# Right-hand matrix loaded before Wv, its casts on GpSimd, its scales spread by two fp32 matmuls, and the FFN of two chunks ahead of V

## The chip, the cores and the metric

The kernel runs on all 8 cores of one Trainium2 chip, each with its own 4096 tokens; the cores don't exchange data. The metric is the device time of the slowest core in microseconds. A profile beside it shows one execution on each core; the numbers below are of its slowest core, 6, where nothing else is said.

## The reference

For x of 16 sequences x 2048 tokens x 1024 features:

```python
xn = _layernorm(x, axis=-1)                       # no gain, no bias
s = _L0_attn_ref(xn, Wq, Wk, Wv, Wo)              # 16 heads of 64, causal window of 128 keys
lhs_scale = absmax(xn, each row) / 127;  rhs_scale = absmax(rhs, each column) / 127
q_lhs = round(xn / lhs_scale);  q_rhs = round(rhs / rhs_scale)     # int8
g = _silu((q_lhs @ q_rhs) * lhs_scale * rhs_scale)
x = x + s * g
```

(The lines on the scales are shortened from the reference's helpers.)

## The kernel before, in words

A core treats its 4096 rows as 32 chunks c of 128 rows (two sequences of 16 chunks). Names of PE groups, with chunk or pair s = c // 2 and half h or quarter g:

- TX: eight 128x128 transposes of the normalized chunk `xnr` into `xnt` (chunks 0 to 5; later chunks are transposed by DMA). TL: the same for the quantized chunk `qlr` into `qlt` (chunks 0 to 3). TR: the same for one 128-row strip of the quantized right-hand matrix into `qrhs` (8 strips).
- Q, K: four quarters for a pair of chunks, 16 matmuls of 256 columns each. V, F, O: two halves for a chunk, 8 matmuls of 512 columns each; F is the product with `qrhs` (the FFN), O the output projection.
- S, A: scores, and probabilities times V, of a chunk in four slots b. Before S of a slot comes the exponential of the slot before (one score buffer `psc`); before A comes the mask on VectorE.

`pe_order` writes PE's order out by hand: a start-up part, then for each chunk four slots, with the groups of `slot_gaps(c)` between the slots. The other engines' programs are written out beside it in the same order of events; each engine runs strictly in order, with semaphores between them. From chunk 2 on, every chunk repeats one pattern.

Around the change. The host passes the right-hand matrix transposed (`rhst`), so a strip i of 128 output columns has its scale in one row each: `rabs(i)` is an absolute maximum over a 128x1024 strip (VectorE), `rscale(i)` four small operations for two strips, `rq(i)` the scaling and rounding on ScalarE, in place, `rcast(i)` the cast to bf16 on VectorE, then TR(i) and its two evacuations. Strips are staged in tiles that the steady loop uses later (`xr`, `gg`, `zz`, `tt`), and cast into `aot`/`ao`. The scales come out one per partition, but `zev` (evacuation of F, `zz<-pj,sm,rsb`) needs them along the free axis in all partitions: `load_rs` writes them to DRAM (`rs_scratch`) and reads them back broadcast into `rsb`. Weights are loaded and cast by DMAs that GpSimd issues (`load_w`: 8 of 256 KB landed, 512 KB read); x and the strips by DMAs of SP's queue. `rstd(c)` is six small GpSimd operations, on which `xn(c)` (normalization, VectorE) waits. `cen(c)`, `amax(c)`, `qp(c)`, `ql(c)` quantize a chunk on ScalarE and VectorE in turn.

Of the kernel before, what the change touches and what calls it, by code (L numbers as in the profile page):

```python
# [890 lines left out]
```

How the kernel before makes its waits and increments, by code:

```python
        def op(fn, sem=None, tag=None, n=1):  # L165
            if tok[0].emit:
                i = fn()
                if sem is not None:
                    i.then_inc(S[sem], n)
            if sem is not None:
                tok[0].add(sem, n, tag)
# [1 line left out]
        def need(eng, sem, tag):  # L173
            if tok[0].emit:
                eng.wait_ge(S[sem], tok[0].named[(sem, tag)])
# [1 line left out]
        def landed(eng, sem, nth):  # L177
            if tok[0].emit:
                eng.wait_ge(S[sem], 16 * (nth + 1))
# [1 line left out]
        def own(eng, sem):  # L181
            if tok[0].emit:
                eng.wait_ge(S[sem], tok[0].count[sem])
```

## Time and profile before

| | |
|---|---|
| time, median of 3 runs | 723.78 us (722.06 to 723.83) |
| time of the profiled execution | 726.37 us |
| its span, slowest core | 724.8 us (cores 721.8 to 724.8) |
| PE busy | 662.3 us, 91% of the span |
| VectorE, ScalarE, GpSimd busy | 470.6, 349.0, 167.5 us |

The time covers a little more than the span of the slowest core. PE's busy share is an average: a stretch of the start and the steady part have to be read apart. The page's slices show the granted TensorE clock in tenths of full speed: 9s nearly everywhere, lower digits only in the first 130 us.

### The profile page before, as it was taken

What the parts mean: (1) busy time and instruction counts of PE and PEld (TensorE: products, weight loads), DVE (VectorE), ACT (ScalarE), POOL (GpSimd) and SP (SyncE); (2) the same over time, 40 slices, a digit from 0 to 9 for tenths busy, and PEclk for the clock granted to TensorE, in tenths of its full rate; (3) what the DMA queues carried; (4) which work ended last, traced back from release to release, by engine and by line L of the source; (5) the groups of instructions that cost most, each with busy time, mean ns of one, the idle gap of its engine ahead of it and who ended that gap; (6) DMA issues with size and microseconds to landing.
All of it is one profiled execution on the core that took longest, in us unless ns stands there. A gap on an engine that the chain in (4) does not pass through costs nothing.

```text
span 724.8 us, 16874 instructions; the slowest of 8 cores (721.8 to 724.8 us)
## 1 busy us (share of the span) xinstructions
PE 662.3 (91%) x5655; PEld 414.1 (57%) x5720; DVE 470.6 (65%) x955; ACT 349.0 (48%) x479; POOL 167.5 (23%) x291
## 2 busy tenths in 40 slices
PE   2879662999999999999999999999999999999985
PEld 2665331666665656666666556566666665656642
DVE  4644651777777667766767766677666677664485
ACT  2634631544455555555445545455554455554442
POOL 7312000132221221222222212112222221220122
PEclk9989976899999999999999999999999999999999
DMA  9999703385454455755544644666465445542343
GB/s 189 183 190 242 133 1 72 74 168 128 109 87 116 113 130 132 132 118 131 129 105 79 117 128 117 131 132 132 117 132 124 99 92 114 121 96 74 74 93 141
DMA packets 111043, 86.92 MB, mean 120 GB/s; under 512 B 93168, under 2 KB 93296, under 8 KB 110960
## 3 DMA queue, kind: packets, MB, share of 16 engines
q1 hardware_dynamic: 106064, 77.35, 47.6%
q0 software_dynamic: 4608, 8.39, 7.7%
q8 instruction: 48, 0.79, 0.5%
q14 instruction: 35, 0.29, 0.2%
q10 hardware_dynamic: 288, 0.10, 0.1%
HBM read 55.15 MB, written 16.78 MB: 99 GB/s over the span
## 4 chain that ended last, share of the span: by engine, by line
PE 81%; DMA 6%; DVE 5%; issue 4%; POOL 2%; ACT 1%; DVEq 0%; POOLq 0%; SPq 0%; ACTq 0%
PE pj L661 42%; PE pj L652 28%; PE psc L743 5%; PE pav L767 4%; DMA xs<-x 2%; DMA rsb<-rs_scratch 2%; PE pav L769 2%; DMA rs_scratch<-sm 2%; DVE ee L353 1%; DVE sm L288 1%; DVE sm L403 1%; POOL wk L811 1%; POOL sm L791 0%; DVE xnr L318 0%; DVE ao L366 0%
## 5 line engine op out<-in xcount | busy, mean ns | idle before, releaser
L559 ACT ACTIVATE ee<-psc 128x1024 bf16<-128x1024 f32 (+1 forms) x128 | 128.3, 1003 | 163.8 <-PE psc L743 153.1
L806 POOL TENSOR_TENSOR xr<-tt,xr 128x512 f32<-128x512 f32 x63 | 80.4, 1278 | 369.4 <-DVE tt L391 338.7
L652 PE MATMUL pj<-xnt,wk 128*128 128x256 bf16 x1024 | 119.6, 277 | 5.0 <-ACT kt L542 4.5
L652 PE MATMUL pj<-xnt,wq 128*128 128x256 bf16 x1024 | 119.8, 276 | 2.2 <-ACT qt L542 1.1
L661 PE MATMUL pj<-qrhs,qlt 128*128 128x512 bf16 x482 | 117.5, 387 | 2.9 <-DVE qrhs L308 1.2
L661 PE MATMUL pj<-wv,xnt 128*128 128x512 bf16 x482 | 115.5, 383 | 1.9 <-issue 0.2
L661 PE MATMUL pj<-wo,aot 128*128 128x512 bf16 x507 | 115.8, 379 | 1.5 <-ACT aot L310 1.2
L353 DVE TENSOR_TENSOR ee<-ee,mask_s 128x1024 bf16<-128x1024 bf16 (+1 forms) x128 | 102.9, 804 | 15.4 <-ACT ee L559 5.9
L652 PEld LDWEIGHTS pj<-xnt,wk 128*128 128x128 bf16 x1024 | 99.6, 99 | 17.7 <-issue 5.4
L652 PEld LDWEIGHTS pj<-xnt,wq 128*128 128x128 bf16 x1024 | 99.4, 99 | 15.1 <-issue 2.9
L661 PEld LDWEIGHTS pj<-wo,aot 128*128 128x128 bf16 x512 | 49.6, 98 | 59.8 <-issue 1.5
L661 PEld LDWEIGHTS pj<-qrhs,qlt 128*128 128x128 bf16 x512 | 48.5, 99 | 55.2 <-issue 4.6
L391 DVE TENSOR_TENSOR tt<-pj,gg 128x512 f32<-128x512 f32 x64 | 44.0, 690 | 53.9 <-PE pj L661 52.7
L525 ACT ACTIVATE xs<-xs,sm 128x1024 f32<-128x1024 f32 x32 | 36.7, 1148 | 83.7 <-DVE xnr L318 83.7
L661 PEld LDWEIGHTS pj<-wv,xnt 128*128 128x128 bf16 x512 | 48.2, 98 | 48.4 <-issue 1.7
L377 DVE SCALAR_TENSOR_TENSOR zz<-pj,sm,rsb 128x512 f32<-128x512 f32 x64 | 47.8, 747 | 30.4 <-DMA rsb<-rs_scratch 20.9
L366 DVE TENSOR_TENSOR ao<-pav,sm 128x256 bf16<-128x256 f32 x128 | 54.4, 425 | 17.9 <-DVE sm L364 5.9
L767 PE MATMUL pav<-vv,ee 128*128 128x65 bf16 x480 | 47.1, 197 | 18.9 <-DVE ee L353 18.3
L323 DVE TENSOR_REDUCE sm<-xs 128x1 f32<-128x1024 f32 x32 | 38.9, 1217 | 35.0 <-ACT xs L525 35.0
L743 PEld LDWEIGHTS psc<-qt,kt 64*128 64x128 bf16 x992 | 28.4, 95 | 51.3 <-issue 51.0
L743 PE MATMUL psc<-qt,kt 64*128 64x128 bf16 x992 | 50.6, 221 | 4.1 <-ACT ee L559 4.1
L767 PEld LDWEIGHTS pav<-vv,ee 128*128 128x128 bf16 x480 | 32.6, 98 | 32.0 <-issue 20.4
(76 smaller groups left out, 616.0 us busy)
## 6 DMA issues: line engine op xcount, KB each, us to landing
xs<-x SPq DMA_DIRECT2D x32, 512.0 KB, 5.6
xr<-x SPq DMA_DIRECT2D x32, 512.0 KB, 6.4
y<-xr SPq DMA_DIRECT2D x31, 512.0 KB, 7.3
wq<-wqt POOLq DMA_DIRECT2D x8, 256.0 KB, 15.5
wk<-wkt POOLq DMA_DIRECT2D x8, 256.0 KB, 19.4
wv<-wvt POOLq DMA_DIRECT2D x8, 256.0 KB, 22.5
xr<-rhst SPq DMA_DIRECT2D x4, 512.0 KB, 7.2
wo<-wot POOLq DMA_DIRECT2D x8, 256.0 KB, 9.7
```

Of the source, the lines that this page charges most:

```text
L323: op(lambda: v.reduce_max(col(c, AMAX), xs[c % XS][:], AX.X, apply_absolute_value=True), "v")
L353: op(lambda: v.tensor_tensor(a, a, m, ALU.mult), "v", ("mask", c, b))
L366: op(lambda: v.tensor_tensor(view(ao[c % 2], b * 256, (64, 4), (1, 64)), view(p, 0, (66, 4), (1, 64)), bass.AP(sm, C_RS + 4 * (b % 2), [[1 ...
L377: op(lambda: v.scalar_tensor_tensor(zz[h], banks[bank["F", c, h]], col(c, LSH), rsb[:, h * 512:(h + 1) * 512], ALU.mult, ALU.mult), "v", ( ...
L391: op(lambda: v.tensor_tensor(tt[h], banks[bank["O", c, h]], gg[c % 2][:, h * 512:(h + 1) * 512], ALU.mult), "v", ("ev", "O", c, h))
L525: op(lambda: a.activation(xs[c % XS][:], xs[c % XS][:], AF.Identity, scale=-1.0, bias=col(c, MEAN)), "a", ("cen", c))
L559: op(lambda: a.activation(o, i, AF.Exp, scale=0.125), "a", ("exp", c, b))
L652: yield [(lambda kc=kc, m=m: t.matmul(p[:, m * 256:(m + 1) * 256], w[:, kc * 1024 + (2 * j + m) * 128:kc * 1024 + (2 * j + m + 1) * 128], ...
L661: yield [lambda kc=kc: t.matmul(p[:], src[:, off + kc * step:off + kc * step + 128], w[:, kc * 1024 + j * 512:kc * 1024 + (j + 1) * 512], ...
L743: todo.append(lambda m=m, kk=kk, ko=ko, rows=rows, q0=q0: t.matmul(psc[:, q0:q0 + 128], kk[rows, m * 256 + ko:m * 256 + ko + 128], qt[s % ...
L767: todo.append(lambda out=out, e0=e0, vp=vp: t.matmul(out, e[:, e0:e0 + 128], vp, start=True, stop=False))
L806: op(lambda: p.tensor_tensor(r, tt[h], r, ALU.add), "p", ("add", c, h))
```

## The change

The work is the same but for the way the scales are spread. What moves:

- SP's queue loads only x of chunks 0 to 3 first, then, once the sixth piece of Wk has landed, the eight strips, then x of chunks 4 to 6.
- GpSimd issues four pieces of Wq before the first `rstd`s and the rest in between; it casts the strips (`rcast`), and issues Wv in two fours between the casts, and Wo after the casts and `rstd(5)`.
- The scales: `rdiag` writes the identity matrix times the scales (diagonal blocks) into `rsb`, a matmul with a matrix of ones sums over the partitions (RS, one for each half), and ScalarE copies the sum over `rsb`.
- PE's order: TR 0 to 3, RS, half 0 of F for chunks 0 and 1, then TR 4 to 7, RS, half 1, all ahead of V. The slots of chunks 0 and 1 hold V of chunks 4 and 5 alone.
- Chunks 4 and 5 are centred and quantized later.

```diff
@@ slot_gaps
-    if c == 0:
-        return [[g] + halves("TR", i) for i, g in enumerate(halves("V", 4, 5))]
-    if c == 1:
-        return [halves("TR", 4, 5), halves("TR", 6, 7) + halves("F", 0)[:1], halves("F", 0, 1)[1:3], f[1:]]
+    if c < 2:
+        v = halves("V", c + 4)
+        return [v[:1], [], v[1:], []]
@@ pe_order
-    out += one(ks("Q", 1)) + one(halves("TL", 0))
-    out += [("G", ks("K", 0), range(8))]
-    out += one(ks("K", 1)) + one(halves("TL", 1, 2))
-    out += [("G", halves("V", 0, 1), range(8))] + one(halves("TX", 4) + halves("V", 2))
-    out += one(halves("TX", 5) + halves("TL", 3) + halves("V", 3))
+    out += one(ks("Q", 1)) + one(halves("TL", 0, 1))
+    out += [("G", ks("K", 0), range(8))] + one(halves("TL", 2))
+    out += one(ks("K", 1)) + one(halves("TL", 3))
+    for h in range(2):
+        out += one(halves("TR", *range(4 * h, 4 * h + 4)) + [("RS", 0, h), ("F", 0, h), ("F", 1, h)])
+    out += [("G", halves("V", 0, 1), range(8))]
+    out += one(halves("TX", 4) + halves("V", 2) + halves("TX", 5) + halves("V", 3))
@@ staging
-        stage = [xr[0], xr[1], xr[2], gg[0], gg[1], zb, tb]
-        rst_bf = [aot[0], aot[1], ao[1]]
+        stage = [gg[0], gg[1], zb, tb, xr[0], xr[1], xr[2], tb]
+        rst_bf = [aot[0], aot[1], ao[0], ao[1]]
@@ emit_sync
-            for c in range(6):
+            for c in range(4):
                 load_x(sync, c)
-            landed(sync, "wv4", 0)
+            landed(sync, "wk5", 0)
             for i in range(8):
                 load_rh(sync, i)
-            t_ql(sync, 4)
-            t_ql(sync, 5)
-            load_x(sync, 6)
-            load_rs(sync)
+            for c in range(4, 7):
+                load_x(sync, c)
@@ VectorE: rcast goes, rdiag is new
+        def rdiag(v, h):
+            need(v, "v", ("rsc", 4 * h + 2))
...
+            op(lambda: v.tensor_tensor(view(rsb, h * 512, (128, 4), (1, 128)), view(ident, 0, (0, 4), (1, 128)),
+                                       bass.AP(sm, C_RST + 4 * h, [[192, 128], [1, 4], [0, 128]]), ALU.mult),
+               "v", ("rdiag", h))
@@ ScalarE
+            elif k == "RS":
+                need(a, "t", g)
+                op(lambda: a.copy(rsb[:, h * 512:(h + 1) * 512], banks[bank[g]]), "a", ("ev",) + g)
@@ PE
+            if k == "RS":
+                yield [lambda: t.matmul(p, ones[:], rsb[:, j * 512:(j + 1) * 512], start=True, stop=True)]
@@ GpSimd
+        def rcast(p, i):
+            need(p, "a", ("rq", i))
+            if i >= 4:
+                need(p, "t", ("TR", i - 4, 1))
+            op(lambda: p.tensor_scalar(rst_bf[i % 4][:], stage[i][:], -MAGIC, 1.0, ALU.add, ALU.mult),
+               "p", ("rcast", i))
```

Three places of the engines' orders. GpSimd, first of the kernel before, from the `rstd` of chunk 3 over Wv to the first operation of chunk 4:

```order
L789 TENSOR_SCALAR sm<-sm 128x1
L791 TENSOR_TENSOR sm<-sm 128x1
L793 TENSOR_TENSOR sm<-sm 128x1
L795 TENSOR_TENSOR sm<-sm 128x1
L797 TENSOR_SCALAR sm<-sm 128x1
L799 TENSOR_TENSOR sm<-sm 128x1
L811 DMA wv<-wvt 128x1024 x8
L789 TENSOR_SCALAR sm<-sm 128x1
```

and of the changed kernel, after the `rstd` of chunk 3 (L839 is `rcast`, L816 the first operation of `rstd(4)`):

```order
L845 DMA wk<-wkt 128x1024 x5
L839 TENSOR_SCALAR aot<-gg 128x1024 x2
L845 DMA wv<-wvt 128x1024 x4
L839 TENSOR_SCALAR ao<-zz 128x1024
L839 TENSOR_SCALAR ao<-tt 128x1024
L845 DMA wv<-wvt 128x1024 x4
L839 TENSOR_SCALAR aot<-xr 128x1024 x2
L839 TENSOR_SCALAR ao<-xr 128x1024
L839 TENSOR_SCALAR ao<-tt 128x1024
L816 TENSOR_SCALAR sm<-sm 128x1
```

Wv now stands behind casts, which wait for ScalarE; before, nothing but `rstd(3)` stood ahead of it.

PE of the kernel before, from K to the first TR (transposes have `ident_s`; L743 is S, L769 A):

```order
L652 MATMUL pj<-xnt,wk 128x256 x128
L646 MATMUL psc<-ident_s,qlr 128x128 x8
L646 MATMUL pav<-ident_s,qlr 128x128 x8
L661 MATMUL pj<-wv,xnt 128x512 x32
L646 MATMUL psc<-ident_s,xnr 128x128 x8
L661 MATMUL pj<-wv,xnt 128x512 x16
L646 MATMUL pav<-ident_s,xnr 128x128 x8
L646 MATMUL psc<-ident_s,qlr 128x128 x8
L661 MATMUL pj<-wv,xnt 128x512 x16
L743 MATMUL psc<-qt,kt 128x128 x4
L661 MATMUL pj<-wv,xnt 128x512 x8
L646 MATMUL pj<-ident_s,aot 128x128 x8
```

and of the changed kernel, from TR(3) to V of chunks 0 and 1 (L666 is RS, `pj<-qrhs,qlt` F):

```order
L671 MATMUL psc<-ident_s,ao 128x128 x8
L666 MATMUL pav<-rsb,ones_s 128x512
L686 MATMUL pj<-qrhs,qlt 128x512 x16
L671 MATMUL pav<-ident_s,aot 128x128 x4
L671 MATMUL psc<-ident_s,aot 128x128 x8
L671 MATMUL pav<-ident_s,aot 128x128 x4
L671 MATMUL pav<-ident_s,ao 128x128 x4
L671 MATMUL psc<-ident_s,ao 128x128 x8
L671 MATMUL pav<-ident_s,ao 128x128 x4
L666 MATMUL pav<-rsb,ones_s 128x512
L686 MATMUL pj<-qrhs,qlt 128x512 x16
L686 MATMUL pj<-wv,xnt 128x512 x32
```

TR, RS and four halves of F now lie between K and V; before, they lay between the slots of chunks 0 and 1.

SP's queue of the kernel before, from its start to the first load of the residual x:

```order
L202 DMA xs<-x 128x1024 x6
L246 DMA xr<-rhst 128x1024 x3
L246 DMA gg<-rhst 128x1024 x2
L246 DMA zz<-rhst 128x1024
L246 DMA tt<-rhst 128x1024
L246 DMA xr<-rhst 128x1024
L223 DMA_TRANSPOSE qlt<-qlr 128x8x128 x2
L202 DMA xs<-x 128x1024
L250 DMA rs_scratch<-sm 128x8x1
L253 DMA rsb<-rs_scratch 128x1024
L229 DMA_TRANSPOSE aot<-ao 128x8x128
L209 DMA xr<-x 128x1024
```

and of the changed kernel:

```order
L203 DMA xs<-x 128x1024 x4
L247 DMA gg<-rhst 128x1024 x2
L247 DMA zz<-rhst 128x1024
L247 DMA tt<-rhst 128x1024
L247 DMA xr<-rhst 128x1024 x3
L247 DMA tt<-rhst 128x1024
L203 DMA xs<-x 128x1024 x3
L224 DMA_TRANSPOSE qlt<-qlr 128x8x128
L230 DMA_TRANSPOSE aot<-ao 128x8x128
L210 DMA xr<-x 128x1024
```

The two transfers by way of `rs_scratch` are gone, and two loads of x have moved behind the strips.

## Rows read from the trace of the kernel before

**Rows 1.** Stretches of the span: length, busy time (instructions) by engine, granted clock, DMA share, GB/s.

```profile
36.00:50.00 14.00, 9.49 (x76) 7.85 (x77) 8.50 (x19) 6.04 (x9) 3.48 (x12) 0.88 1.06 177
50.00:58.00 8.00, 8.00 (x64) 6.56 (x63) 0.02 (x1) 2.63 (x5) 0.00 (x0) 0.78 1.04 264
58.00:75.00 17.00, 16.60 (x104) 8.39 (x104) 10.08 (x18) 8.57 (x15) 4.34 (x8) 1.00 1.05 216
112.00:126.00 14.00, 0.00 (x0) 0.00 (x0) 1.82 (x5) 1.08 (x2) 0.00 (x0) 0.61 0.48 94
200.00:690.00 490.00, 487.44 (x4213) 303.86 (x4262) 333.74 (x668) 248.09 (x340) 110.97 (x180) 1.00 0.53 113
```

**Rows 2.** The chain that ended last: start us, us, what.

```profile
94.53 14.62 DMA rs_scratch<-sm
109.22 14.69 DMA rsb<-rs_scratch
```

**Rows 3.** Timeline of PE: start us, us, line, operation [idle before <- releaser].

```profile
27.92 7.15 PE L652 MATMUL pj<-xnt,wq 128*128 128x256 bf16 x64 [1.14 <-ACT qt L542]
47.65 10.00 PE L652 MATMUL pj<-xnt,wk 128*128 128x256 bf16 x64 [4.51 <-ACT kt L542]
58.79 6.85 PE L661 MATMUL pj<-wv,xnt 128*128 128x512 bf16 x31 [0.25 <-issue]
...
74.08 0.29 PE L743 MATMUL psc<-qt,kt 64*128 64x128 bf16 x4
...
103.79 3.19 PE L661 MATMUL pj<-qrhs,qlt 128*128 128x512 bf16 x7 [1.23 <-DVE qrhs L308]
...
107.89 3.74 PE L661 MATMUL pj<-qrhs,qlt 128*128 128x512 bf16 x16
...
126.30 0.22 PE L767 MATMUL pav<-vv,ee 128*128 128x65 bf16 x1 [14.35 <-DVE ee L353]
...
130.24 0.61 PE L743 MATMUL psc<-qt,kt 64*128 64x128 bf16 x8
```

**Rows 4.** Timeline of ScalarE.

```profile
45.30 1.15 ACT L525 ACTIVATE xs<-xs,sm 128x1024 f32<-128x1024 f32 x1 [1.62 <-DVE xnr L318]
...
71.35 2.21 ACT L536 ACTIVATE xr<-xr,sm 128x1024 f32<-128x1024 f32 x2
...
131.00 1.02 ACT L559 ACTIVATE ee<-psc 128x1024 bf16<-128x1024 f32 x1 [2.31 <-PE psc L743]
```

**Rows 5.** Timeline of VectorE.

```profile
41.30 0.81 DVE L318 TENSOR_SCALAR xnr<-xs,sm 128x1024 bf16<-128x1024 f32 x1
...
83.08 1.21 DVE L403 TENSOR_REDUCE sm<-zz 128x1 f32<-128x1024 f32 x1
84.40 0.17 DVE L409 TENSOR_SCALAR sm<-sm 128x2 f32<-128x2 f32 x1
...
85.01 0.17 DVE L414 TENSOR_SCALAR sm<-sm 128x2 f32<-128x2 f32 x1
...
90.48 0.68 DVE L420 TENSOR_SCALAR aot<-gg 128x1024 bf16<-128x1024 f32 x1
...
124.08 0.75 DVE L377 SCALAR_TENSOR_TENSOR zz<-pj,sm,rsb 128x512 f32<-128x512 f32 x1 [20.91 <-DMA rsb<-rs_scratch]
```

**Rows 6.** Timeline of GpSimd.

```profile
21.91 0.19 POOL L789 TENSOR_SCALAR sm<-sm 128x1 f32<-128x1 f32 x1 [2.66 <-DVE sm L290]
...
41.49 0.67 POOL L789 TENSOR_SCALAR sm<-sm 128x1 f32<-128x1 f32 x1 [1.09 <-DVE sm L290]
...
62.63 4.34 POOL L811 DMA_DIRECT2D wo<-wot  x8 [18.42 <-DMA gg<-rhst]
...
142.76 1.27 POOL L806 TENSOR_TENSOR xr<-tt,xr 128x512 f32<-128x512 f32 x1 [5.74 <-DVE sm L364]
```

**Rows 7.** Wk's loads: issue (first and last start), then time from issue to landing.

```profile
L811 POOL DMA_DIRECT2D wk<-wkt x8: 535/571/797, 12.1 to 16.0; - x8
...
DMA to landing us min/median/max: 14.3/19.4/25.9
```

**Rows 8.** Wv's loads, the same.

```profile
L811 POOL DMA_DIRECT2D wv<-wvt x8: 547/562/874, 24.4 to 28.5; - x8
...
DMA to landing us min/median/max: 18.8/22.5/25.8
```

More of the change, by code:

```diff
@@ L207, in load_xr @@
             elif c < 3:
-                need(sync, "v", ("rcast", 7))
+                need(sync, "p", ("rcast", 7))
             op(lambda: sync.dma_start(xr[c % XR][:], x_h[c * 128:(c + 1) * 128, :]), f"lr{c % XR}", c, 16)
@@ L372, in zev @@
             if c == 0:
-                landed(v, "rsr", 0)
-                need(v, "v", ("rcast", 7))
+                emptied(v, ("RS", 0, h))
+                need(v, "p", ("rcast", 3))
             else:
@@ L388, in t1 @@
             need(v, "v", ("g", c, h))
-            if c:
-                need(v, "p", ("add", c - 1, h))
+            need(v, "p", ("add", c - 1, h) if c else ("rcast", 7))
             op(lambda: v.tensor_tensor(tt[h], banks[bank["O", c, h]], gg[c % 2][:, h * 512:(h + 1) * 512],
@@ L451, in emit_vector @@
             ql(v, 0)
+            amax(v, 1)
+            ql(v, 1)
             amax(v, 2)
[L453 to L454 removed]
             evac_v(v, ("TL", 0, 0))
             ql(v, 2)
[L457 to L462 removed]
+            amax(v, 3)
             evac_v(v, ("TL", 1, 0))
+            ql(v, 3)
             evac_v(v, ("TL", 2, 0))
[L465 to L466 removed]
             rabs(v, 0)
[L468 removed]
             rabs(v, 1)
             rscale(v, 0)
[L471 to L481 removed]
+            evac_v(v, ("TL", 3, 0))
+            rabs(v, 2)
+            rabs(v, 3)
+            rscale(v, 2)
+            rdiag(v, 0)
+            evac_v(v, ("TR", 0, 0))
+            evac_v(v, ("TR", 1, 0))
+            rabs(v, 4)
+            evac_v(v, ("TR", 2, 0))
+            rabs(v, 5)
+            rscale(v, 4)
+            evac_v(v, ("TR", 3, 0))
+            rabs(v, 6)
+            zev(v, 0, 0)
+            rabs(v, 7)
+            rscale(v, 6)
+            rdiag(v, 1)
+            gate(v, 0, 0)
+            zev(v, 1, 0)
+            evac_v(v, ("TR", 4, 0))
+            evac_v(v, ("TR", 5, 0))
+            gate(v, 1, 0)
+            evac_v(v, ("TR", 6, 0))
+            evac_v(v, ("TR", 7, 0))
+            bn(v, 4)
+            zev(v, 0, 1)
+            xn(v, 4)
+            gate(v, 0, 1)
+            zev(v, 1, 1)
+            bn(v, 5)
+            xn(v, 5)
+            gate(v, 1, 1)
+            evac_v(v, ("TX", 4, 0))
+            evac_v(v, ("TX", 5, 0))
+            extra = {(0, 1): [(amax, 4)], (0, 3): [(ql, 4)], (1, 1): [(amax, 5)], (1, 3): [(ql, 5)]}
             held, gates = None, []
@@ L507, in emit_vector @@
                         ql(v, c + 4)
[L508 to L509 removed]
+                    todo = [g for g in gap if evacuator(g) == "v"]
+                    if b == 3 and todo:
                         held = todo.pop()
@@ L676, in pe_ready @@
             if k == "TR" and j == 0:
-                need(t, "v", ("rcast", i))
+                need(t, "p", ("rcast", i))
+            if k == "RS":
+                need(t, "v", ("rdiag", j))
             if k == "TA":
@@ L814, in emit_gpsimd @@
         def emit_gpsimd(p):
-            for w in range(3):
-                load_w(p, w)
-                rstd(p, 2 * w)
-                rstd(p, 2 * w + 1)
-            landed(p, "rh4", 0)
-            load_w(p, 3)
+            load_w(p, 0, range(4))
+            rstd(p, 0)
+            rstd(p, 1)
+            load_w(p, 0, range(4, 8))
+            load_w(p, 1, range(3))
+            rstd(p, 2)
+            rstd(p, 3)
+            load_w(p, 1, range(3, 8))
+            rcast(p, 0)
+            rcast(p, 1)
+            load_w(p, 2, range(4))
+            rcast(p, 2)
+            rcast(p, 3)
+            load_w(p, 2, range(4, 8))
+            for i in range(4, 8):
+                rcast(p, i)
+            rstd(p, 4)
+            rstd(p, 5)
+            load_w(p, 3, range(8))
             held = None
```

122 lines of the change are left out of this document (50 added, 72 removed).

## The prediction

> **What bounds the kernel now.** I read the stretches of the span first. From 200 to 690 us PE is busy for 487.44 of 490 us at full clock [rows 1]: the steady part is PE's, the change doesn't touch it, and what can be won lies before chunk 2. PE's timeline puts the first scores of chunk 2 at 130.24 us [rows 3]; what follows (724.8 - 130.2 = 594.6 us) I leave as it is. The question is when chunk 2 can start in the changed kernel.
>
> The chain of waits shows what holds it in the kernel before: the write of the scales to DRAM takes 14.62 us and the broadcast read back 14.69 us, one after the other from 94.53 to 123.9 us [rows 2]. The first `zev` waits 20.91 us for it [rows 5], and PE, which finds its work in the meantime until 112 us, stands still for 14.35 us [rows 3]; the stretch from 112 to 126 has no PE work at all [rows 1]. A smaller stall lies earlier: PE waits 4.51 us before K of pair 1 [rows 3], because ScalarE's `cen(4)` and `cen(5)` stand ahead of the evacuations of K and wait for late chunks of x (the last ran from 45.30 [rows 4]); after it K ran 10.00 us where the same 64 matmuls of Q took 7.15 [rows 3], with the clock at 0.78 in that stretch [rows 1]. The transfers are the other limit of the start: their share is about 1.0 through 75 us [rows 1]. Wk's last piece was issued at 16.0 and landed up to 25.9 us later, at 41.9 [rows 7]; Wv's last at 28.5 + 25.8 = 54.3 [rows 8]. Eight pieces in 12.4 us is 1.55 us for 512 KB read; I use 1.6.
>
> **The change, step by step.** I follow the longest chain from K to chunk 2, in the times of core 6.
>
> *K.* Loads of x for chunks 4 and 5 no longer share the engines with Wk: two units of 1.6 us less, of which the first strips (issued at the sixth piece) take about one back. Wk's last piece then lands at 40, K of pair 0 ends at 41 (it ended at 47.65 - 4.51 = 43.1), pair 1 starts after one evacuation, at 41.7, since `cen(4)` and `cen(5)` are behind; at Q's 7.15 us it ends at 48.9, where before it ended at 57.65. The strips 0 and 1 land by about 41, and `rabs` (1.21 us each) and `rscale` (84.40 to 85.2, 0.8 us) [rows 5] are done before 45. Beside PE, they cost nothing.
>
> *First four casts.* ScalarE's `rq(0)` stands behind the last evacuation of K, so it starts at 49.5 and takes 2.21 / 2 = 1.1 us [rows 4]; the casts start at 50.7. No row shows a GpSimd operation of 1024 columns. From below: not under the 0.68 us that VectorE needs for the same cast [rows 5], and `rq` feeds one only each 1.1 us. The nearest row is GpSimd's add of 512 columns, 1.27 us, with two inputs read [rows 6]; its 128x1 operation takes 0.19. By elements read, 1024 of one input cost the same 1.27; by elements written, 0.19 + 2 x 1.08 = 2.35, rounded up to the double of the row, 2.5. I take 1.3 us: casts 0 and 1 end at 53.3. Issuing eight pieces of weights takes 4.34 us [rows 6], so four of Wv take 2.2 and hold the casts until 55.7; casts 2 and 3 end at 58.3 (their `rq`s, after `rabs` and `rscale` behind the evacuation of TL(3), end by 55). TR(3) is done at 58.9.
>
> *RS and F, half 0.* An fp32 matmul is in no row. At least it costs the 512-column bf16 one at full clock (3.74 / 16 = 0.23 us), at most I allow four passes at half clock, 4 x 3.19 / 7 = 1.8 us [rows 3]. I take the long end, 1.7, since PE has been nearly idle since 49 us. TR(3)'s evacuation and ScalarE's copy of RS lie under it and under F. F of chunk 0 starts at 60.6 and costs 3.4 us at half clock (3.19 for 7 recorded); chunk 1 takes 2.6, between that and 1.9 at full clock (3.74 for 16): PE is at 66.6.
>
> *Last four casts.* `zev(0,0)` stands on VectorE ahead of `rabs(7)` and `rscale(6)`: 64.0 + 0.8 + 1.2 + 0.9 = 66.9. Then `rq(6)` to 68.0, cast 6 to 69.4, cast 7 to 70.7, TR(7) and its evacuation to 71.3, RS 1.3 (PE's clock unsure again), F of half 1 at 2.6 and 2.0: 77.2. The casts 4 and 5 and TR(4) to TR(6) lie under this.
>
> *V.* Wv's first piece starts at about 54.3; twelve units (eight of Wv, strip 7, three of x) end at 54.3 + 12 x 1.6 = 73.5, before V needs them at 77.2. The old stretch from V to the first scores took 74.08 - 58.79 = 15.3 us with 0.5 of TL(3) in it [rows 3]; V of chunks 0 to 3 ends at 92.0.
>
> *Slots of chunks 0 and 1.* A slot can't be shorter than scores, exponential and start of the next: for chunk 1, 0.6 + 1.02 + 0.2 = 1.9 us [rows 3, 4], for chunk 0, with half the columns, 1.2. Four slots also hold a half of V, 1.9 us beside 0.3 to 0.7 of scores and A. So 2.2 + 1.2 + 2.5 + 1.2 for chunk 0 and 2.6 + 1.9 + 2.8 + 1.9 for chunk 1, 16.3 us; `amax`, `ql` and `qp` of chunks 4 and 5 push the masks and exponentials of single slots by up to 1: 17. Chunk 2 starts at 109.
>
> What is hidden: Wo is issued after `rstd(5)`, at about 82, and its eight units land by 97, ahead of O of chunk 0 at 113. `rcast` leaves VectorE, eight times 0.68 us [rows 5], beside the path.
>
> The gain is 130.2 - 109 = 21.2 us. The profiled execution took 726.4 and would take 705.2; the median of the runs shown, 723.8, is 2.6 below it, and the same gain from there gives 702.6. I say 703.
>
> *A cost from sharing.* GpSimd's first operation of `rstd(5)` took 0.67 us at 41.49, and 0.19 elsewhere [rows 6]; it ended at 42.16, as VectorE's `xn` ran from 41.30 to 42.11 [rows 5]. So the two hold each other up. In the casts' window VectorE has `rdiag` and `gate` with two inputs in SBUF; one of each held for a cast is 2 x 1.3 = 2.6 us, or nothing where PE waits elsewhere. I put nothing in the sum and up to 2.6 in the range. The Trainium skill has this as a rule (SBUF — State Buffer, "Who interferes with whom"): an instruction of VectorE with two SBUF inputs contends with a GpSimd instruction that reads SBUF, and the one that issues second fully blocks. [...] The sum by the rule would be up to 705.6, by the row at its best 703.
>
> **The rivals.**
>
> *Slow casts* (chance 0.15): GpSimd needs 2.5 us for one. Six casts lie one behind the other in the chain (0 to 3, 6 and 7), so 6 x 1.2 = 7.2 us more: 710, from 708 to 714. For it speaks that the only large row of GpSimd is slow; against it, that this row reads two inputs.
>
> *Fast casts, warm PE* (0.19): the casts keep pace with `rq`, 1.1 us (6 x 0.2 = 1.2 less), PE holds its clock over the gaps (1.5 us less at each half of F, 0.8 at RS), and the slots run 2 us closer: 1.2 + 3.8 + 2 = 7, so 696, from 693 to 698. For it speaks that from 58 to 75 us the clock stayed at 1.00 [rows 1]; against it, the loss of clock after only 4.51 us of idle. The Trainium skill (GPSIMD Engine Reference, "4.1 Engine selection") says of this that elementwise work belongs on VectorE, but that one-input operations run at about line rate on GpSimd; 1024 columns at its 1.2 GHz would be an estimate of about 1 us. No row here shows it.
>
> *Wv or a strip comes late* (0.06): between cast 1 and the first piece of Wv the queues run dry from about 49 to 54 us; if the later loads run at 2.3 us a unit, V waits from 77 to 82 and more. 708 to 716.
>
> *Slower than before* (0.02): Wo, now issued behind all casts and `rstd(5)`, holds O of chunk 0. Its place is the second slot of chunk 2, at 113; it eats the whole gain only if Wo lands 21 us after that, at 134, when it is 52 us behind its issue. Before, it was issued at 62.63 and needed at 139; the longest wait of a weight from issue to landing was 25.9 us [rows 7], so this would need double that: 724 to 730.
>
> *The forecast* has 0.58, with a range of its own from 698 to 708.
>
> **How the numbers follow.** 703 is the likeliest case. The range must leave out no more than 2 in 10: from 695 to 711 it holds the forecast, two thirds of the fast case, half of the slow casts and half of the late transfers. Differences under 0.3%, about 2 us, can't be told from no change here. All cases but the last gain more; the last gives 0.02 slower, and 0.01 stands for the same.
>
> **What would show it.** The casts' mean on GpSimd (1.3, or 2.5); the end of K of pair 1 (48.9); the start of the first F (60.6) and of V (77.2); the first scores of chunk 2 (109), where the gain must stand whole, with the rest at 594 us; granted clock between 50 and 77 us. The prediction is wrong if V waits for Wv, if O waits for Wo, or if the steady part moves.

## The result and the profile after

The changed kernel takes 726.41 us (median of its runs, 725.17 to 727.36) against 723.78 us before; the ratio is 1.0042, with a 95% interval from 1.0026 to 1.0058. It is slower by 0.4%. The forecast was 703 us, in a range from 695 to 711. (Of seven runs of each kernel one, at 839 and at 770 us, fell in a slower state of the chip, for the changed kernel with one die at a clock of 0.81; without such runs, which the ratios, the range and all times below leave out, the medians are 726.0 and 723.1.)

The profiled execution took 726.41 us with a span of 724.1 on core 7. The head of its page and two of its rows by slices of 18 us:

```profile
span 724.1 us, 16956 instructions; the slowest of 8 cores (718.2 to 724.1 us)
PE   2696697999999999999999999999999999999995
PEclk9896898999999999999999999999999999999999
```

What differs lies in the first seven slices, where PE's digits are 2696697 for 2879662 before: the nearly empty seventh slice is gone, and the second and the fourth are emptier than they were. The same stretches as in [rows 1], and two more, from the view by windows (PE, PEld, DVE, ACT and POOL busy; then granted clock, DMA share, GB/s):

```profile
36.00:50.00 14.00, 13.96 (x134) 12.32 (x132) 3.82 (x9) 4.92 (x8) 0.00 (x0) 0.97 0.84 248
50.00:58.00 8.00, 7.86 (x79) 6.98 (x78) 3.24 (x7) 3.91 (x9) 0.00 (x0) 1.00 0.11 44
58.00:75.00 17.00, 10.94 (x53) 5.46 (x50) 10.87 (x20) 10.09 (x14) 10.42 (x14) 0.60 0.70 114
75.00:90.00 15.00, 8.86 (x54) 4.75 (x52) 10.90 (x21) 8.01 (x12) 3.60 (x8) 0.89 0.63 152
112.00:126.00 14.00, 10.45 (x81) 4.40 (x79) 8.40 (x25) 7.00 (x9) 0.00 (x0) 0.76 0.35 76
200.00:690.00 490.00, 490.00 (x4254) 303.36 (x4254) 335.45 (x668) 246.97 (x339) 110.02 (x181) 1.00 0.52 113
```

From 112 to 126 us PE now works for 10.45 us where it had nothing to do [rows 1]: the round trip through DRAM is gone. But from 58 to 90 it idles for 12.2 of 32 us, and the clock is 0.60 in the first 17, where it did V at full clock [rows 1]. The transfers, with a share of about 1.0 up to 75 us before [rows 1], nearly stop from 50 to 58. PE's timeline at the places that the prediction named (start, duration, line, what, and in brackets the idle time before and what ended it):

```profile
33.11 8.91 PE L677 MATMUL pj<-xnt,wq 128*128 128x256 bf16 x64 [4.76 <-ACT qt L550]
...
50.69 7.15 PE L677 MATMUL pj<-xnt,wk 128*128 128x256 bf16 x64
57.67 0.61 PE L671 MATMUL psc<-ident_s,qlr 128*128 128x128 bf16 x8
60.91 1.01 PE L671 MATMUL pav<-ident_s,aot 128*128 128x128 bf16 x8 [2.63 <-POOL aot L839]
...
65.12 1.01 PE L671 MATMUL pav<-ident_s,ao 128*128 128x128 bf16 x8 [2.17 <-DVE sm L393]
...
66.93 2.02 PE L666 MATMUL pav<-rsb,ones_s 128*128 128x512 f32 x2
70.19 5.63 PE L686 MATMUL pj<-qrhs,qlt 128*128 128x512 bf16 x16 [1.24 <-ACT qrhs L303]
...
80.53 0.38 PE L671 MATMUL pav<-ident_s,ao 128*128 128x128 bf16 x4 [3.81 <-DVE qrhs L301]
...
90.11 8.75 PE L686 MATMUL pj<-wv,xnt 128*128 128x512 bf16 x32 [2.05 <-DVE zz L368]
...
106.75 0.29 PE L770 MATMUL psc<-qt,kt 64*128 64x128 bf16 x4
...
127.88 0.40 PE L770 MATMUL psc<-qt,kt 64*128 64x128 bf16 x8 [1.47 <-ACT ee L567]
```

K of pair 1 ends at 57.7, as before (47.65 + 10.00 [rows 3]); the forecast was 48.9. The first scores of chunk 2 start at 127.9, not 109, and the rest takes 724.1 - 127.9 = 596.2 us. Against the forecast chain, the 18.9 us split by these rows into 8.8 up to the end of K, 0.8 from there to the first F (12.5 for 11.7), 3.3 from F to V (19.9 for 16.6), 1.8 from V to the first scores (16.6 for 14.8) and 4.1 in the slots of chunks 0 and 1 (21.1 for 17).

Why K is late is seen on the two engines ahead of it. VectorE and ScalarE of the changed kernel, the rows of `amax` of chunks 0 and 1 (L316, the absolute maxima), `qp` of both (L538, the scaling that needs them) and the evacuations of Q of pair 0 (L550):

```profile
23.61 1.21 DVE L316 TENSOR_REDUCE sm<-xs 128x1 f32<-128x1024 f32 x1
28.17 1.21 DVE L316 TENSOR_REDUCE sm<-xs 128x1 f32<-128x1024 f32 x1
...
26.31 1.15 ACT L538 ACTIVATE xs<-xs,sm 128x1024 f32<-128x1024 f32 x1 [4.12 <-DVE sm L324]
30.43 1.15 ACT L538 ACTIVATE xs<-xs,sm 128x1024 f32<-128x1024 f32 x1 [1.47 <-DVE sm L324]
31.95 2.05 ACT L550 CAST qt<-pj 128x512 bf16<-128x512 f32 x4
```

In the repeated run of the kernel before (below) the same three of ScalarE are:

```profile
19.62 1.15 ACT L530 ACTIVATE xs<-xs,sm 128x1024 f32<-128x1024 f32 x1 [2.05 <-DVE sm L331]
25.85 1.15 ACT L530 ACTIVATE xs<-xs,sm 128x1024 f32<-128x1024 f32 x1 [1.57 <-DVE sm L331]
28.70 2.05 ACT L542 CAST qt<-pj 128x512 bf16<-128x512 f32 x4
```

The change puts `bn(3)` (the statistics of chunk 3), `xn(2)` and `xn(3)` ahead of `amax(0)` on VectorE; `amax(0)` now starts at 23.61, where the `qp(0)` that needs it had started at 19.62. ScalarE's `qp(0)` and `qp(1)` wait for `amax`, and the evacuations of Q of pair 0 stand behind both. They start 3.2 us later, PE waits 4.76 us for them, and Q of pair 1 then starts at 33.11 for 27.92 and runs 8.91 us for 7.15 [rows 3]: 7.0 us are lost here, about what the change wins behind it (the 4.51 us of waiting before K and the 2.85 us by which K ran longer than Q).

GpSimd and VectorE of the changed kernel in the casts' window (L399 is a small step of `rscale`; L375 is `gate`, which works on the result of F with two inputs in SBUF):

```profile
59.72 2.07 POOL L839 TENSOR_SCALAR aot<-gg 128x1024 bf16<-128x1024 f32 x2 [33.77 <-ACT gg L544]
61.74 2.16 POOL L845 DMA_DIRECT2D wv<-wvt  x4
63.88 1.10 POOL L839 TENSOR_SCALAR ao<-zz 128x1024 bf16<-128x1024 f32 x1
64.89 1.09 POOL L839 TENSOR_SCALAR ao<-tt 128x1024 bf16<-128x1024 f32 x1
...
80.18 1.04 POOL L839 TENSOR_SCALAR ao<-tt 128x1024 bf16<-128x1024 f32 x1
...
60.95 0.87 DVE L399 TENSOR_SCALAR sm<-sm 128x2 f32<-128x2 f32 x1
67.47 0.17 DVE L399 TENSOR_SCALAR sm<-sm 128x2 f32<-128x2 f32 x1
78.40 0.68 DVE L375 SCALAR_TENSOR_TENSOR gg<-gg,zz 128x512 f32<-128x512 f32 x1
80.78 0.98 DVE L375 SCALAR_TENSOR_TENSOR gg<-gg,zz 128x512 f32<-128x512 f32 x1 [0.17 <-ACT gg L573]
```

A cast takes 1.04 to 1.10 us. The prediction's estimate of about 1 us agrees with these rows; it rests on what the Trainium skill (GPSIMD Engine Reference, "4.1 Engine selection") says of operations with one input on GpSimd, that they run at roughly line rate.

### The profile page after: what moved, and what is told of

The parts are those of the page before. It is cut to its first block, busy times and chain, and to the rows that moved or that the text cites. A ratio compares the mean times of both kernels' runs of the same rounds, so it can differ in the third digit from the quotient of the medians.

```text
span 724.1 us, 16956 instructions; the slowest of 8 cores (718.2 to 724.1 us)
## 1 busy us (share of the span) xinstructions
PE 671.9 (93%) x5724; PEld 415.3 (57%) x5724; DVE 471.7 (65%) x950; ACT 351.2 (49%) x481; POOL 173.5 (24%) x299
## 4 chain that ended last, share of the span: by engine, by line
PE 85%; DVE 4%; DMA 3%; issue 3%; POOL 2%; ACT 2%; DVEq 0%; SPq 0%; POOLq 0%; ACTq 0%
PE pj L686 44%; PE pj L677 29%; PE psc L770 5%; PE pav L794 3%; PE pav L796 2%; DMA tt<-rhst 1%; DMA xs<-x 1%; DVE ee L346 1%; DMA aot<-ao 1%; DVE sm L281 1%; DVE sm L316 1%; ACT ee L567 0%; PE psc L671 0%; POOL sm L818 0%; DVE xnr L311 0%
## 5 line engine op out<-in xcount | busy, mean ns | idle before, releaser
L677 PE MATMUL pj<-xnt,wq 128*128 128x256 bf16 x1024 | 122.2, 279 | 7.7 <-ACT qt L550 4.8
L686 PE MATMUL pj<-wv,xnt 128*128 128x512 bf16 x512 | 124.7, 390 | 2.1 <-DVE zz L368 2.1
L686 PE MATMUL pj<-qrhs,qlt 128*128 128x512 bf16 x512 | 122.6, 384 | 1.2 <-ACT qrhs L303 1.2
L677 PE MATMUL pj<-xnt,wk 128*128 128x256 bf16 x1024 | 116.7, 273 | 0.2
L346 DVE TENSOR_TENSOR ee<-ee,mask_s 128x1024 bf16<-128x1024 bf16 (+1 forms) x128 | 105.2, 822 | 11.0 <-ACT ee L567 5.6
L357 DVE TENSOR_TENSOR ao<-pav,sm 128x256 bf16<-128x256 f32 x128 | 54.4, 425 | 17.7 <-DVE sm L355 5.8
L316 DVE TENSOR_REDUCE sm<-xs 128x1 f32<-128x1024 f32 x32 | 39.0, 1218 | 35.0 <-ACT xs L533 35.0
L550 ACT CAST qt<-pj 128x512 bf16<-128x512 f32 x64 | 35.7, 583 | 33.0 <-PE pj L677 33.0
L550 ACT CAST kt<-pj 128x512 bf16<-128x512 f32 x64 | 35.7, 583 | 31.0 <-PE pj L677 31.0
## 6 DMA issues: line engine op xcount, KB each, us to landing
wk<-wkt POOLq DMA_DIRECT2D x8, 256.0 KB, 12.5
```

The source lines that it names most:

```text
L316: op(lambda: v.reduce_max(col(c, AMAX), xs[c % XS][:], AX.X, apply_absolute_value=True), "v")
L346: op(lambda: v.tensor_tensor(a, a, m, ALU.mult), "v", ("mask", c, b))
L357: op(lambda: v.tensor_tensor(view(ao[c % 2], b * 256, (64, 4), (1, 64)), view(p, 0, (66, 4), (1, 64)), bass.AP(sm, C_RS + 4 * (b % 2), [[1 ...
L550: op(lambda: a.copy(dst[:, g * 512:(g + 1) * 512], banks[bank[k, s, g]]), "a", ("ev", k, s, g))
L677: yield [(lambda kc=kc, m=m: t.matmul(p[:, m * 256:(m + 1) * 256], w[:, kc * 1024 + (2 * j + m) * 128:kc * 1024 + (2 * j + m + 1) * 128], ...
L686: yield [lambda kc=kc: t.matmul(p[:], src[:, off + kc * step:off + kc * step + 128], w[:, kc * 1024 + j * 512:kc * 1024 + (j + 1) * 512], ...
```

## The experiments

Starts of stages given below are means over the eight cores of one profiled execution, so that one core's late start doesn't decide; "chunk 2" is the start of the first matmul of Q in its first slot, and the end of K is given as the start of K's last matmul. From chunk 2 to the end of the span, that mean is 593.3 to 595.8 us in all of these kernels: the start of chunk 2 sets the time, to within 2.5 us. Each ratio is to the kernel before as it was timed beside that experiment, with its 95% interval. "The changed kernel" is the one predicted. The kernel before took 723.1 us beside it and 722.1 to 722.6 us beside the experiments, so a difference in us between the changed kernel and an experiment can be about 1 us too large; the difference of the ratios, which is free of that, is given too where it matters.

**1. The kernel before once more.** No edit.

> The kernel before, unchanged. The changed kernel's slowest core starts chunk 2 about 3 us earlier than the profiled run of the kernel before, yet its median time is 2.6 us longer. Theory A (the profiled run of before was one of its slower ones, as its 726.4 us beside a median of 723.8 says): here the slowest core's span is 720 to 722.5 us and the first scores of chunk 2 come at 126 to 129 us. Rival B (the changed kernel loses later, in the steady part): the first scores come at 130 again, and the time is 722 to 724. The ratio to itself is 1.000 within 0.002.

Measured: 721.9 us, ratio 0.9996 (0.9987 to 1.0005), as Theory A has it. The profiled execution has a mean span of 719.4 us, and chunk 2 at 126.1; the one that the prediction used had 723.8 and 130.2. PE's waits from 30 to 130 us (us in total, times, longest), and the first scores of chunk 2:

```profile
PE pav L767 <- DVE ee L353: 9.0, 1, 9.0
PE pj L646 <- ACT vv L548: 5.5, 2, 4.0
PE pj L652 <- ACT kt L542: 3.9, 1, 3.9
...
126.48 0.40 PE L743 MATMUL psc<-qt,kt 64*128 64x128 bf16 x8
```

And the two transfers of the scales, in the chain that ended last:

```profile
95.81 18.38 DMA rs_scratch<-sm
114.24 5.91 DMA rsb<-rs_scratch
```

The stall for the scales is 9.0 us here (5.8 to 10.2 over the cores), not the 14.35 of [rows 3]. The two transfers take 24.3 us together, and 24.3 to 24.8 on all eight cores, for the 29.3 of [rows 2]; what made them slower in that execution no run shows. The trace that the prediction read had the warning in it: on its cores 0 to 2 the same stall is 8.7 to 9.1 us, and the 14.35 is the longest single one of its eight cores. An execution 4 us late at that place was the baseline of the whole sum: from 126.5 in place of 130.2 the same forecast of 109 gives a gain of 17.5 us and, from the median of 723.8, a time of about 706. And the changed kernel, with chunk 2 at a mean of 126.3, starts it no earlier than this one does: what it gains at the scales is spent in full before chunk 2. Most of what makes it slower than before lies behind that. Its mean span is 721.0 us for 719.4, and of the difference 0.9 us falls in chunks 2 and 3 and 0.5 us behind the start of chunk 28, while from chunk 4 to 28 both take 480.69 us; its slowest core is 3.1 us above that mean for 2.0. No experiment looks into that.

**2. The matmuls alone.** The kernel before, with the round trip replaced as in the change, and nothing else moved:

```diff
-    return [halves("TR", 4, 5), halves("TR", 6, 7) + halves("F", 0)[:1], ...
+    return [halves("TR", 4, 5), halves("TR", 6, 7) + halves("RS", 0) + halves("F", 0)[:1], ...
-            load_rs(sync)
```

`rdiag` stands on VectorE behind `rscale(2)` and `rscale(6)`, and ScalarE copies the result of RS, as in the change.

> The kernel before with one part of the change: the scales are spread by rdiag, two fp32 matmuls and ScalarE's copy in place of the two transfers; the matmuls stand behind TR of strip 7. Theory A: the round trip by DRAM costs what the chain of before shows after 112 us (14 us of PE's idle time, some 2 to 3 us of F and scores at half clock), so chunk 2 starts at 112 to 116 and the time is 706 to 710. Rival B (the start of chunk 2 doesn't set the end, or the next wait in line is close behind): 716 to 724.

Measured: 713.95 us, ratio 0.9886 (0.9870 to 0.9902); chunk 2 at 115.1, F at 105.6. The start of chunk 2 is where Theory A put it and 11.0 us earlier than in experiment 1, but the time falls by only 8 us and misses both ranges. The mean span gains 10.4 us (709.0 for 719.4); the slowest core is 3.1 us above that mean here and 2.0 in experiment 1, and the time 2.1 us above the slowest span for 1.5. Why the cores lie further apart no run shows. PE's places behind the removed wait:

```profile
98.11 0.38 PE L653 MATMUL pj<-ident_s,aot 128*128 128x128 bf16 x4 [4.05 <-ACT vv L550]
103.84 3.75 PE L648 MATMUL pj<-rsb,ones_s 128*128 128x512 f32 x4 [0.54 <-DVE qrhs L300]
```

The matmuls themselves take 3.75 us for both halves, at a granted clock near 0.5. One of the change's parts thus makes the kernel 1.1% faster; all the others together cost 11 to 12 us (726.0 - 714.0 = 12.0 us, or 11.3 us by the ratios 1.0042 and 0.9886; chunk 2 at 126.3 for 115.1).

**3. `qp(1)` behind the evacuations of Q.** The changed kernel, ScalarE:

```diff
-            qp(a, 1)
             evac_a(a, ("TX", 3, 1))
             for g in range(4):
                 ev_qk(a, "Q", 0, g)
+            qp(a, 1)
```

> The changed kernel with ScalarE's qp(1) moved behind the evacuations of Q of pair 0. Theory A (that order cost 4 to 5 us of waiting and 1.8 us of half clock before Q of pair 1, and all later steps hang on it): Q of pair 1 starts at 29 to 30, K of pair 1 ends at 50 to 53, chunk 2 starts 5 to 7 us earlier, time 719 to 722. Rival B (the strips or Wv set the later steps, so the gain is waited away before V): K ends early but V starts at 88 to 90 as now, time 725 to 727.

Measured: 723.2 us, ratio 1.0015 (1.0005 to 1.0026). K of pair 1 ends at 54.4 (57.3 in the changed kernel) and chunk 2 starts at 123.1 (126.3). The 3 us are still there at chunk 2, and 2.0 (by the ratios) to 2.9 us of them in the time: ScalarE's order ahead of K is one cost, about half as large as Theory A had it. `qp(0)`, still ahead and waiting for the late `amax(0)`, was left: PE waits 3.6 us at that place here, in one wait on the slowest core.

**4. The empty slots filled.** The changed kernel, with V of chunks 2 and 3 taken from ahead of the slots into the two empty slots of chunks 0 and 1 (and `halves("V", 2)`, `halves("V", 3)` left out of the stretch ahead):

```diff
-        v = halves("V", c + 4)
-        return [v[:1], [], v[1:], []]
+        v, w = halves("V", c + 4), halves("V", c + 2)
+        return [v[:1], w[:1], v[1:], w[1:]]
```

> The changed kernel with V of chunks 2 and 3 moved from the start-up into the empty slots 1 and 3 of chunks 0 and 1. Theory A (the eight slots took 21 us for 7 us of V and 8 of scores and products, because half of them hold no filler and PE falls to half clock): slots with V in each take no longer than now, the 7 us of V before them go, chunk 2 starts 5 to 7 us earlier, time 719 to 722. Rival B (the slots are as long as PE's work in them; moving V only moves it): time 725 to 727.

Measured: 719.7 us, ratio 0.9970 (0.9955 to 0.9984), as Theory A has it; chunk 2 at 120.4, 5.9 us earlier, though it starts V no earlier (90.0 for 89.6). In the time that is 5.2 us by the ratios and 6.4 by the medians. The first scores of chunk 0 and of chunk 2 in PE's timeline:

```profile
102.60 0.29 PE L768 MATMUL psc<-qt,kt 64*128 64x128 bf16 x4 [2.00 <-ACT xnt L303]
...
122.29 0.40 PE L768 MATMUL psc<-qt,kt 64*128 64x128 bf16 x8
```

The slots hold four more halves of V (1.89 us each at full clock) and last 19.7 us, where the changed kernel's last 21.1: the empty ones had only waited for exponentials and masks. In the slots of the changed kernel PE waits 4.4 us for exponentials and 1.9 for masks; here it waits 0.9 us for masks and for exponentials in no case. Two of the halves of V that the changed kernel has there ran slow behind such waits, 3.17 and 3.50 us at granted clocks of 0.66 and 0.62 in the stretches around them. From the changed kernel, the wait for exponentials and the first of the two:

```profile
PE psc L770 <- ACT ee L567: 4.4, 4, 1.5
...
116.05 3.17 PE L686 MATMUL pj<-wv,xnt 128*128 128x512 bf16 x8
```

**5. A tile of its own for strip 7.** The changed kernel; the last strip doesn't wait for a cast:

```diff
-        stage = [gg[0], gg[1], zb, tb, xr[0], xr[1], xr[2], tb]
+        stage = [gg[0], gg[1], zb, tb, xr[0], xr[1], xr[2], st7]
-            if i == 7:
-                need(sync, "p", ("rcast", 3))
```

> The changed kernel with a tile of its own for strip 7 of the right-hand matrix, so that SP's queue no longer waits for the cast of strip 3 before it loads strip 7 and x of chunks 4 to 6; these four loads fall into the stretch in which the queues ran dry. Theory A (strip 7 landed at 75.5 us, and PE waited 3.8 us for its scale): strip 7 lands by 56, that wait goes, V starts 3 to 4 us earlier, time 722 to 724. Rival B (the last four casts wait for the evacuation of F anyway): V starts at 88 to 90, time 725 to 727.

Measured: 724.83 us, ratio 1.0033 (1.0021 to 1.0046), chunk 2 at 124.6. The interval overlaps that of the changed kernel (1.0026 to 1.0058), so a gain in the time isn't shown; chunk 2 is 1.7 us earlier. The strip's landing was on the chain of the changed kernel (a row of the view that follows it back, start and duration):

```profile
66.05 9.43 DMA tt<-rhst
```

but with it early, V starts at 88.9 for 89.6, as Rival B has it: at the transposes of strip 6 PE still waits 2.8 us (3.81 in the changed kernel), and ahead of V 1.9 us for `zev` (2.05), each on the slowest core.

**6. The three mends together.**

> The changed kernel with the three edits together: Q's evacuations ahead of qp(1), V of chunks 2 and 3 in the empty slots, a tile of its own for strip 7. Theory A (the losses lie one behind the other, so the gains add): 3 us, 6 us and 3 us less, 711 to 715, at or below the kernel with the matmuls alone (714). Rival B (each edit uncovers the next wait): 716 to 720.

Measured: 714.88 us, ratio 0.9894 (0.9878 to 0.9909), as Theory A has it, 10.7 (by the ratios) to 11.2 us faster than the changed kernel. V starts at 85.8, chunk 2 at 116.1: that is 10.2 us earlier, where the three alone sum to 3.2 + 5.9 + 1.7 = 10.8. So these three places hold nearly all of the 11 to 12 us. The time can't be told from experiment 2's (0.9886): the rest of the rearrangement, mended so, wins nothing either. The stretch ahead of V remains: PE is busy for 21.26 of 30 us from 60 to 90 at a clock of 0.75, and for 24.76 of 28 at 1.00 behind it:

```profile
60.00:90.00 30.00, 21.26 (x102) 9.86 (x101) 18.59 (x36) 15.18 (x21) 12.24 (x24) 0.75 0.47 71
90.00:118.00 28.00, 24.76 (x211) 12.31 (x210) 16.02 (x41) 17.66 (x26) 4.77 (x9) 1.00 0.76 114
```

**7. Wv ahead of the casts.** The changed kernel; GpSimd issues all of Wv right behind Wk:

```diff
-            rcast(p, 0)
-            rcast(p, 1)
-            load_w(p, 2, range(4))
-            ...
+            load_w(p, 2, range(8))
+            for i in range(8):
+                rcast(p, i)
```

> The changed kernel with all eight pieces of Wv issued right behind Wk, ahead of GpSimd's casts. Theory A (the casts hold Wv back until 62 us, the queues run dry from 52 to 62, and strip 7 then shares the engines with Wv): Wv lands by about 65, strip 7, issued at 64 to 66, lands 3 us after its issue, and V starts 2 to 4 us earlier: 722 to 724. Rival B (Wv, now sharing with the strips, holds these up by more than is won): F starts later than 70 and the time is 726 to 729.

Measured: 724.16 us, ratio 1.0027 (1.0013 to 1.0041); F at 70.0, V at 88.4, chunk 2 at 124.4. The interval overlaps the changed kernel's; V starts 1.2 us earlier, below the 2 to 4 of Theory A, and Rival B's later F isn't there. The idle queues cost little: in both kernels PE's last wait ahead of V is for `zev`, about 2 us, and none is for Wv.

**8. The casts on VectorE.** Experiment 7 with `rcast` as before the change, on VectorE; for it `rabs(2)`, `rabs(3)` stand one place earlier, and `rabs(4)`, `rabs(5)`, `rscale(4)` behind the evacuations of TR(2) and TR(3).

> As the kernel with Wv ahead of the casts, with the eight casts back on VectorE (0.68 us in place of 1.04 us) and the absolute maxima of strips 2 and 3 ahead of the evacuation of TL 3. Theory A (where the casts run doesn't matter: two of them lie in the chain before each group of TR): F starts 0 to 2 us earlier, time within 2 us of the kernel with Wv ahead of the casts. Rival B (GpSimd's casts were the slow step of the start-up): V starts 4 us earlier or more.

Measured: 728.75 us, ratio 1.0084 (1.0063 to 1.0106), 4.6 us slower than experiment 7; F at 70.3 (70.0), V at 91.7 (88.4). Neither expectation had that. In this order, where VectorE has `rabs`, evacuations and `zev` in one short stretch, the casts on GpSimd are 4.6 us better although one takes half as long again there (1.04 for 0.68 us). The steps moved with the casts have a share in it that wasn't measured.

**9. Before, with matmuls, and `cen` out of the way.** Experiment 2, and the small stall of [rows 3] mended on ScalarE:

```diff
             evac_a(a, ("TL", 0, 1))
-            cen(a, 4)
-            cen(a, 5)
             for g in range(4):
                 ev_qk(a, "K", 0, g)
-            qp(a, 4)
-            qp(a, 5)
+            cen(a, 4)
+            cen(a, 5)
             for g in range(4):
                 ev_qk(a, "K", 1, g)
+            qp(a, 4)
+            qp(a, 5)
```

> The kernel before with the matmuls for the scales, and ScalarE's cen(4) and cen(5) moved behind the evacuations of K of pair 0. Theory A (in the old order these two cost PE 3.4 to 4.5 us before K of pair 1 and 2 to 3 us of half clock in it, and nothing after hides it): K of pair 1 ends at 50 to 53 instead of 55 to 58, and the time is 3 to 6 us below the kernel with the matmuls alone, 708 to 711. Rival B (V then waits for Wv, which lands at 54, and the strips, which set the slots of chunks 0 and 1): V starts at 55 at the earliest and the slots still wait for the strips: 713 to 715.

Measured: 708.83 us, ratio 0.9818 (0.9805 to 0.9830), as Theory A has it. K of pair 1 ends at 51.6 (56.6 in experiment 2) and chunk 2 starts at 110.0 (115.1), all 5 us kept. No wait for Wv appears. What PE waits for most up to chunk 2, besides the start:

```profile
PE pj L653 <- ACT vv L550: 5.6, 2, 4.0
...
PE psc L752 <- ACT ee L561: 3.0, 2, 2.7
```

**10. V back between K and TR, with the mends.** Experiment 6 with Wv right behind Wk and V of chunks 0 and 1 ahead of the transposes:

```diff
     out += one(ks("K", 1)) + one(halves("TL", 3))
+    out += [("G", halves("V", 0, 1), range(8))]
     for h in range(2):
         out += one(halves("TR", ...) + [("RS", 0, h), ("F", 0, h), ("F", 1, h)])
-    out += [("G", halves("V", 0, 1), range(8))]
```

> The changed kernel with the three mends, and V of chunks 0 and 1 put back between K and the strips' transposes, with Wv issued right behind Wk. Theory A (with F ahead of V, PE has nothing to do from K's end to the first F, some 12 us of which V of chunks 0 and 1 would fill 7, and TR and F run at half clock): F starts 0 to 2 us later than in the three mends (65 to 69), the 7 us of V behind F go, and so does some half clock: 706 to 709. Rival B (V holds the evacuations and the casts back by as much as it fills): 713 to 716.

Measured: 717.85 us, ratio 0.9947 (0.9928 to 0.9966), 3 us slower than experiment 6 and above both expectations. PE's timeline of it:

```profile
60.12 1.02 PE L685 MATMUL pj<-wv,xnt 128*128 128x512 bf16 x4 [1.55 <-DMA wv<-wvt]
...
63.08 1.87 PE L685 MATMUL pj<-wv,xnt 128*128 128x512 bf16 x4 [1.93 <-DMA wv<-wvt]
...
72.45 2.77 PE L685 MATMUL pj<-qrhs,qlt 128*128 128x512 bf16 x6 [2.90 <-ACT rsb L582]
...
95.61 1.01 PE L670 MATMUL pav<-ident_s,xnr 128*128 128x128 bf16 x8 [5.93 <-DVE xnr L310]
```

V now waits for Wv, which shares the queues with the strips, F starts 3.9 us later (70.7 for 66.8), and where V had stood PE finds `xn(5)` not done, for 5.93 us: V had covered the late loads of x. The first scores of chunk 0 come at 95.9 for 95.7, so what V won ahead of F is lost by then; chunk 2, at 118.0 for 116.1, loses 1.9 us more in the slots.

**11. The same in the changed kernel without the mends.** Wv stands right behind Wk here too, so experiment 7 is the one to compare with.

> The changed kernel with that one edit: V of chunks 0 and 1 between K and the strips' transposes, Wv issued right behind Wk, the rest as changed. Theory A: 5 to 9 us less than the changed kernel, 717 to 721. Rival B (V waits for Wv, which now shares the engines with the strips, and pushes F back by as much): 724 to 727.

Measured: 720.9 us, ratio 0.9984 (0.9970 to 0.9998), as Theory A has it: 3.3 us faster than experiment 7, and 4.2 (by the ratios) to 5.2 us faster than the changed kernel; chunk 2 at 121.0 (124.4 and 126.3). The sign is the opposite of experiment 10's. PE's waits, as means over the cores, show what differs. In both, V takes the place of PE's waits ahead of the first strips, ahead of the third and for `zev` (2.7, 2.2 and 1.9 us in experiment 6, nearly the same in experiment 7), which the mends had not shortened. But PE's wait for `xn` of chunks 4 and 5 is 2.6 us here and 6.2 in experiment 10: V of chunk 2, which the second mend moves into the slots, still stands here between the two chunks' transposes. Experiment 10 waits for Wv besides (1.0 us).

**12. The best kernel with its casts on GpSimd.** Experiment 9, `rcast` moved to GpSimd behind the issue of Wo:

```diff
             load_w(p, 3)
+            for i in range(8):
+                rcast(p, i)
```

> The kernel of the experiment before with the two additions to before (scales by fp32 matmul, cen(4) and cen(5) behind K's evacuations), which took 708.8 us, and its eight casts moved from VectorE to GpSimd, as the change does, and nothing else moved. Theory A (the casts are not what bounds the start of chunk 2 there: PE's waits in its slots are for ScalarE, 5.6 us for vv and 3.0 for ee, and a cast is 1.04 us on GpSimd against 0.69 on VectorE): no difference that can be told, 707 to 710. Theory B (VectorE is the pacemaker of the slots, and 8 x 0.69 = 5.5 us less of it bring masks and evacuations forward): 704 to 706.5. Theory C (a chain of rq, cast, TR paced by the slower cast and by strip 7, which waits for cast 0): F of chunk 0 and with it chunk 2 start 1 to 3 us later, 710 to 712.

Measured: 707.8 us, ratio 0.9795 (0.9768 to 0.9822), as Theory A has it; chunk 2 at 109.2 for 110.0. The intervals of 9 and 12 overlap, so a gain by the casts isn't shown here; a loss is unlikely. Both are the fastest of this study, about 2% faster than the kernel before and some 2.4% faster than the changed one. The casts cost the same as in the changed kernel (busy us, mean ns, idle before):

```profile
L812 POOL TENSOR_SCALAR aot<-gg 128x1024 bf16<-128x1024 f32 x2 | 2.1, 1044 | 7.1 <-ACT gg L529 7.1
```

## Why the prediction was wrong

*What bounds the kernel.* Right in kind: the steady part didn't move (PE busy for 490.00 of 490 us, the rest 596.2 for 594.6 us), and the start of chunk 2 decides. Wrong in size: the chain of waits and PE's idle 14.35 us were read from one core of one execution. Experiment 1 has 9.0 us there, and experiment 2 turned them into 8 us of time. This is worth 3.7 us of the miss, the difference of the two executions at chunk 2; 18.9 us more lie in the chain to chunk 2, which was forecast at 109 and came at 127.9.

*"K of pair 1 ends at 48.9."* This step failed most, by 8.8 us, nearly half of the 18.9 us by which chunk 2 is late. The prediction moved `cen(4)` and `cen(5)` off K's path, as the change does, and kept Q as it was; it never priced the other moves in the same lists, `amax(0)` and `amax(1)` behind `xn(3)` on VectorE, with `qp` on ScalarE waiting for them ahead of Q's evacuations. The wait of 4.51 us before K [rows 3] became one of 4.76 us before Q. Experiment 3 gets 3 us of it back by one line; experiment 9 shows that the stall's removal is worth 5 us where nothing else is moved.

*Casts at 1.3 us.* They take 1.04 to 1.10, the fast case's price. That rival's 696 us didn't come: of its conditions, only the price held, and PE's clock did not (0.60 from 58 to 75 us). The slow casts (710) are refuted; in experiment 8, the one arrangement tried, casts on VectorE made the kernel slower.

*RS and F.* F started 12.5 us after K for 11.7; one fp32 matmul (recorded as two instructions) took 2.02 us, a little above the bound of 1.8 and the 1.7 in the sum; F's 16 matmuls took 5.63 us for the 6.0 of the sum, so the low clock there was foreseen.

*V at 77.2.* F to V took 3.3 us more. Strip 7 was counted as one of twelve units of 1.6 us; it waited for cast 3 and took 9.43 us to land while Wv used the queues, and PE waited 3.81 us. `zev(1,1)`, behind `xn(4)` on VectorE, was named by no step and cost 2.05. Experiment 5 shows that strip 7 alone is no price: with it early, V starts 0.7 us and chunk 2 1.7 us earlier.

*V to the slots.* The old stretch of 15.3 us was taken over as if its clock came with it. V now follows a wait and runs 8.75 us for its first 32 matmuls, against 3.61 for 16 later, which makes 1.5 of the 1.8 us.

*Slots at 17 us.* 21.1, because a slot with nothing in it lasts as long as ScalarE's exponential, VectorE's mask and the starts between them. The floor of 1.2 to 1.9 us was taken for the duration. Before, these gaps held V and transposes; moving that work ahead shortened nothing. Experiment 4 is worth 5.2 to 6.4 us, the largest single mend.

*The sharing of GpSimd and VectorE.* Put at nothing with up to 2.6 us in the range: the rows show 1.0 us, and whether it reaches the end wasn't measured.

*The rivals.* Wv didn't bind (in experiment 7 its early issue moves V by 1.2 us), Wo neither: it was issued at 93.9 to 97.8, not at 82, and landed by 111.4, ahead of O at 138. The time of 726.4 us does lie in the range of the case slower than before (724 to 730, chance 0.02), but that is chance: its only mechanism was O waiting for Wo, and O didn't wait for it. What came true was a sum of lists: each engine's order ahead of the moved block was changed too, and the two prices measured alone are 3 us (the evacuations of Q) and 6 us (the empty slots) at chunk 2. All the other cases, 0.98 together, rested on there being no such cost.

What stays open: `qp(0)`'s share of K's lateness, and the clock's share in the 11 to 12 us, were not measured alone. PE's wait of 4.0 us for `vv` in experiment 9, at the first transposes of TR, was left in place.

## What to carry to other kernels

A stall's length on one core of one execution isn't its price: read it on all cores and in a second execution before it becomes the base of a sum. When a diff moves a block, price every line of the lists that moved with it, above all what now stands ahead of an evacuation that PE waits for. And work taken out of the gaps of a loop that waits for other engines, and put ahead of it, is paid for twice, once where it runs and once where the gap stays; here the change's one good part was worth 8 us alone, and its rearrangement cost 11 to 12.
